# A four-layer conditioned transformer on one core: layer 0's value and output projections merged into one weight, one ScalarE pass per gelu and modulation, a Newton root, and a new order of steps

## The chip, the cores and the metric

The kernel runs on 1 core of one Trainium2 chip. The metric is device time in microseconds (us), the median of several executions. TensorE (PE) does matmuls and transposes into PSUM, VectorE (DVE), ScalarE (ACT) and GpSimd (POOL) work on tiles of 128 partitions, and SyncE (SP) issues the DMAs. Each engine works through its own queue in order and waits on semaphores.

## The reference

Four blocks follow each other on x of shape (4, 512, 256), each conditioned on a vector of 256 per batch. All have the same skeleton, in float32:

```python
def block(x, cond):                # layers 0..3 differ in norm, modulation, gates and heads
    h = modulate(norm(x), cond)    # scale and shift from cond @ W (+ bias)
    q, k, v = h @ Wq + bq, h @ Wk + bk, h @ Wv + bv
    p = softmax(q @ k.T * scale)   # layer 0: 1 head of 256; layers 1 to 3: 16 heads of 16
    x = x + gate * ((p @ v) @ Wp + bp)
    h = modulate(norm(x), cond)
    return x + gate * (gelu(h @ W1 + b1) @ W2 + b2)
```

Layer 0 has an rms norm and no gates. Layer 1 divides q and k by their norms (`x / max(sqrt(sum(x*x)), 1e-12)` over each head's 16 values) and scales q by exp(min(scale_mul, log 100)). Layer 3 has no FFN: its output is its second modulated norm added to x.

## The kernel before

A job is one batch of one layer, so there are 16 (`JOBS`): jobs 0 to 3 are layer 0, 4 to 7 layer 1, and so on. Weights and activations are kept as a rounded high part and the rest (`_h`, `_l`, type fp32r), and a product is three matmuls (`product`, L597 to L599: high by high, high by low, low by high). A few products stay in plain fp32, which TensorE does in two passes: `av0`, `av`, and the small modulation products.

All steps of all jobs stand in one list, `PLAN`, which `plan_steps` sorts by times written in tables (`SINGLE0`, `FFN`, `ATTN`, `LEAD_IN`, ...), in ticks counted from a job's start; a tick is four scores tiles of a unit of four heads. Every engine walks that list and issues its own part of each step, so the list fixes the order in each queue but not when a thing runs. In the windows of multi-head jobs (`multi_window`), the scores and row maxima stand in pairs, and `PAIR` and its kin say where in two ticks the `av` steps (A, or a and b) and the other steps (0 and 1) are put among them.

TensorE writes to a ring of seven PSUM banks (`RING`, `claim`), used in turn by every step of `RINGED`; a bank is claimed again when the engine that reads it has signalled. The eighth bank, `AVB`, holds the `av` sums of multi-head jobs.

What the change touches:
- `av0` and `proj` in layer 0. `pT0` transposes the probabilities into `oU`; `av0` (L729) makes (p v)^T, two tiles of 128x512; ScalarE (L916) rounds it into `postT_h` and VectorE (L1077) makes `postT_l`; `proj` multiplies by `wp`, and VectorE adds the result to X (L1242).
- `hT1`, `hT2`: four transposes, then ScalarE applies scale and shift twice from PSUM (L827), once in full (`hT_f`, `postT_f`) and once rounded (`hT_h`, `postT_h`), and POOL subtracts (L1301). `hT_f` lies in the memory of `hT_l`.
- `gelu`: for each of four tiles of `fc1`, ScalarE applies gelu twice from PSUM (L957, `gT_f` and `gT_h`), and POOL subtracts (L1306) and signals `g_lo`, for which `fc2a` and `fc2` wait.
- `qkroot` and `qkrs` in layer 1: VectorE clips the sums of squares (L1139), ScalarE takes the root (L861), VectorE the reciprocal (L1143) and the scaling of q (L1145).
- The row maxima of layers 2 and 3 (`max`, L1203) on VectorE, the exponentials (`scores`, L891 and L888) on ScalarE. ScalarE loads another function table whenever exp, gelu or sqrt follow each other.
- At the start VectorE splits the three pieces of layer 0's q, k and v weights itself (L1023, L1024; `EARLY`).

## Time and profile before

| what | value |
|---|---|
| three runs | 1158.63, 1163.27, 1162.45 us; median 1162.45 |
| profiled execution | span 1160.9 us from first to last instruction; its time outside the span is not listed apart |
| mean granted TensorE clock | 0.983 of full |
| busy in the span | TensorE 1094.3, ScalarE 800.4, VectorE 706.6, POOL 491.9 us |
| windows of 16 ticks | layer 0 with the lead-in 229.3 us; then 86.0, 84.0, 83.1, 73.9 (scores of layer 1); 84.1, 84.7, 83.0, 82.7 (layer 2); 82.6, 58.2, 58.5 (layer 3) and 70.8 to the end |

The windows are cut at the first scores matmul of each job. A window holds the attention of its job and the out projection and FFN of the job before, and the q, k and v of the job after. A matmul's row gives a modelled end, and neighbours overlap, so the distance from start to start tells what one costs TensorE. The name in a row is that of the tile; buffer numbers are left out.

### The profile page before, as it was taken

The numbers are of one execution on the slowest core, as the hardware profiler recorded it, in microseconds if no ns is written. First come the engines' busy times: TensorE is split into PE (matmuls) and PEld (weight loads), VectorE is DVE, ScalarE is ACT, GpSimd is POOL, SyncE is SP. The second block draws the span as 40 slices with busy tenths as digits, with TensorE's granted clock in tenths as the row PEclk, the third lists the DMA queues.
The fourth block names the chain that finished last, engine by engine and source line by source line (L and its number), as shares of the span: only waits on it lengthen the run. The fifth ranks groups of instructions, "written<-read, shape, count | busy, mean of one in ns | idle before, by whom it ended". The sixth has DMA issues, their size and how long they took to land.

```text
span 1160.9 us, 19685 instructions
## 1 busy us (share of the span) xinstructions
PE 1094.3 (94%) x6717; PEld 703.3 (61%) x6717; DVE 706.6 (61%) x1484; ACT 800.4 (69%) x1336; POOL 491.9 (42%) x447
## 2 busy tenths in 40 slices
PE   8899999889898999999999999999999999999985
PEld 5576877655555565656657656566656566555442
DVE  6554447535256266234775865865865866898874
ACT  3563655477788778787687686687687686686763
POOL 3542742613543623644335553335344345254222
PEclk9999999899999999999999999999999999999997
DMA  7000001213222203321122231023031121232301
GB/s 234 20 26 28 2 10 31 62 38 94 60 64 73 75 1 82 84 58 35 28 75 73 69 83 42 15 65 82 23 88 29 39 55 51 56 84 55 83 12 36
DMA packets 36385, 64.45 MB, mean 56 GB/s; under 512 B 7208, under 2 KB 22312, under 8 KB 36288
## 3 DMA queue, kind: packets, MB, share of 16 engines
q1 hardware_dynamic: 36288, 63.20, 20.6%
q8 instruction: 56, 0.92, 0.3%
q14 instruction: 41, 0.34, 0.1%
HBM read 22.90 MB, written 2.12 MB: 22 GB/s over the span
## 4 chain that ended last, share of the span: by engine, by line
PE 73%; DVE 10%; ACT 8%; issue 6%; POOL 4%; POOLq 0%; ACTq 0%; DVEq 0%
PE rings L597 13%; PE AVB L709 13%; PE rings L598 11%; PE rings L599 11%; PE rings L696 10%; PE rings L671 5%; DVE m L1203 2%; PE rings L729 2%; ACT probs L891 2%; PE rings L734 2%; PE rings L640 1%; ACT L891 1%; DVE m L1183 1%; ACT gT_h L957 1%; PE rings L746 1%
## 5 line engine op out<-in xcount | busy, mean ns | idle before, releaser
L1203 DVE TENSOR_REDUCE m<-rings 128x1 fp32r<-128x512 f32 x512 | 319.0, 681 | 100.6 <-PE rings L671 73.3
L891 ACT ACTIVATE probs<-rings 128x512 f32<-128x512 f32 x562 | 292.9, 616 | 99.4 <-PE rings L671 71.1
L696 PE MATMUL rings<-SQ,SK 64*128 64x512 f32 x768 | 237.9, 446 | 14.7 <-ACT probs L888 6.3
L671 PE MATMUL rings<-SK,SQ 63*128 63x512 f32 x512 | 200.3, 457 | 5.4 <-ACT probs L891 4.2
L696 PEld LDWEIGHTS rings<-SQ,SK 64*128 64x128 f32 x768 | 109.0, 188 | 142.4 <-issue 55.1
L709 PE MATMUL AVB<-probs,V 128*32 128x512 f32 x1536 | 193.6, 611 | 0.0
L1306 POOL TENSOR_TENSOR gT_l<-gT_f,gT_h 128x512 fp32r<-128x512 f32 x96 | 121.4, 1286 | 75.7 <-ACT gT_h L957 73.8
L888 ACT ACTIVATE probs<-rings 128x1024 f32<-128x1024 f32 x103 | 101.0, 1037 | 34.2 <-PE rings L696 20.6
L597 PE MATMUL rings<-w_h,gT_h 128*128 128x256 f32 x384 | 110.2, 287 | 1.2 <-ACT gT_h L957 0.7
L671 PEld LDWEIGHTS rings<-SK,SQ 63*128 63x128 f32 x512 | 84.2, 184 | 39.7 <-ACT probs L891 33.1
L598 PE MATMUL rings<-w_l,gT_h 128*128 128x256 f32 x384 | 106.7, 278 | 0.0
L599 PE MATMUL rings<-w_h,gT_l 128*128 128x256 f32 x384 | 106.7, 278 | 0.0
L957 ACT ACTIVATE gT_f<-rings,colv 128x512 f32<-128x512 f32 x96 | 66.9, 697 | 31.3 <-PE rings L599 28.6
L709 PEld LDWEIGHTS AVB<-probs,V 128*32 128x32 f32 x1536 | 39.5, 109 | 75.1 <-issue 59.8
L597 PE MATMUL rings<-postT_h,w_h 128*128 128x512 f32 x192 | 79.6, 415 | 3.5 <-ACT gT_h L957 2.4
L1301 POOL TENSOR_TENSOR postT_l<-postT_f,postT_h 128x512 fp32r<-128x512 f32 x24 | 31.4, 1310 | 115.4 <-ACT postT_h L827 115.1
L597 PEld LDWEIGHTS rings<-w_h,gT_h 128*128 128x128 f32 x384 | 72.3, 188 | 12.2 <-issue 7.3
L1340 POOL TENSOR_TENSOR tmp<-tmp,gates 128x512 f32<-128x512 f32 x32 | 41.1, 1285 | 86.0 <-DVE tmp L1270 44.9
L598 PE MATMUL rings<-postT_l,w_h 128*128 128x512 f32 x192 | 76.7, 399 | 0.0
L599 PE MATMUL rings<-postT_h,w_l 128*128 128x512 f32 x192 | 76.3, 398 | 0.0
L1301 POOL TENSOR_TENSOR hT_l<-hT_f,hT_h 128x512 fp32r<-128x512 f32 x30 | 38.6, 1290 | 86.7 <-ACT hT_h L827 86.6
L1270 DVE TENSOR_TENSOR tmp<-rings,rowp 128x512 f32<-128x512 f32 x40 | 27.5, 688 | 75.6 <-PE rings L599 75.5
(185 smaller groups left out, 2229.4 us busy)
## 6 DMA issues: line engine op xcount, KB each, us to landing
SQ<-qh SPq DMA_DIRECT2D x96, 128.0 KB, 2.6
SK<-kh SPq DMA_DIRECT2D x96, 128.0 KB, 2.8
SQ<-ql SPq DMA_DIRECT2D x48, 128.0 KB, 2.7
SK<-kl SPq DMA_DIRECT2D x48, 128.0 KB, 2.9
raw<-in_w SPq DMA_DIRECT2D x20, 256.0 KB, 2.8
wmod_s<-in_wmod SPq DMA_DIRECT2D x6, 512.0 KB, 4.1
gates<-gate_rows SPq DMA_DIRECT2D x12, 256.0 KB, 3.6
raw<-in_wqkv SPq DMA_DIRECT2D x9, 256.0 KB, 2.8
```

The source lines that it names most:

```text
L597: pe.matmul(out, sh, mh, start=first, stop=False)
L598: pe.matmul(out, sh, ml, start=False, stop=False)
L599: return pe.matmul(out, sl, mh, start=False, stop=last)
L671: mm = pe.matmul(o[:, :], SQ[a % 4][r:r + KS, n // 2, c * P:(c + 1) * P], SK[a % 4][r:r + KS, n // 2, :], start=True, stop=True)
L696: mm = pe.matmul(o[:, :], SK[a % 4][r:r + KS + 1, n // 2, c * P:(c + 1) * P], SQ[a % 4][r:r + KS + 1, n // 2, :], start=True, stop=True)
L709: mm = pe.matmul(AVB[32 * n:32 * n + 32, :], V[j % 2][:, i, (HD + 1) * h:(HD + 1) * h + 32], probs[:, (4 * t + n) % PROBS, :], start=(i == ...
L888: act.activation(probs[:, n % PROBS:n % PROBS + 2, :], two_banks(kind, a, i), ACT.Exp, scale=SCALE[layer(unit_job(a))]).then_inc(done["sco ...
L891: act.activation(probs[:, n % PROBS, :], bank(kind, a, i)[:, :], ACT.Exp, scale=SCALE[layer(unit_job(a))]).then_inc(done["scores"], 1)
L957: ins = act.activation(dst[:, m % (MT // 2), :], bank("fc1", a, m)[:, :], ACT.Gelu, bias=colv[:, layer(a), col:col + 1])
L1203: nc.vector.tensor_reduce(m16[:, col:col + 1], bank(kind, a, i)[:, :], AX_X, ALU.max, negate=True).then_inc(done["max"], 1)
L1301: nc.gpsimd.tensor_tensor(lo, full, hi.bitcast(F32), ALU.subtract).then_inc(done[kind], 1)
L1306: nc.gpsimd.tensor_tensor(gT_l[:, m, :], gT_f[:, m, :], gT_h[:, m, :].bitcast(F32), ALU.subtract).then_inc(g_lo, 1)
```

## The change

1. Layer 0 no longer multiplies p v by Wp. The third piece of its weights is loaded transposed, and a new step `merge` makes WvWp once (12 matmuls of 128x256, rounded by ScalarE, low part by VectorE) and puts it in Wv's place. `v` is then V WvWp, and `proj` multiplies the transposed probabilities by it (16 fp32 matmuls of 256 columns a job, 32 passes) and gives token-major output at once. `av0` goes. A step `mergerow` (8 passes) adds bv Wp to the bias row.
2. For layers 0 to 2 ScalarE makes only the full tile of hT and gelu. VectorE rounds it (`tensor_copy` to fp32r), and POOL's subtraction waits for that (`rounded`, `g_hi`). Layer 3 keeps both passes.
3. Layer 1's root is made on VectorE: an integer seed and three Newton steps, 12 instructions on 128x128 numbers, after which comes the scaling. Its scratch `root` lies in the memory of `tok1`, which is `kbar`'s too.
4. Until the first multi-head scores the ring has eight banks (`BANK`, `BEFORE`).
5. Every number in the tables of places is another one, so that steps stand elsewhere in the list everywhere.

```diff
+ROOT_SEED, ROOT_STEPS = 0x5f3759df, 3
...
-FFN = {"hT2": (23.5, 23.91), "fc1": (25.6, 25.81, 25.82, 25.83, 29.55, 29.56, 29.57, 29.58), "gelu": (25.84, 29.59),
-       "fc2a": (27.45, 29.55), "fc2": (30.55, 31.2)}
+FFN = {"hT2": (23.77, 23.78), "fc1": (24.07, 24.63, 24.66, 24.92, 28.07, 28.09, 28.15, 28.3), "gelu": (24.95, 29.13),
+       "fc2a": (26.1, 27.16), "fc2": (31.26, 32.12)}
...
+FIRST_SCORES = USE[("scores", UNITS * BATCH, 0)]
+BANK, BEFORE, _users = [], [], {}
+for _n, _s in enumerate(USES):
+    if _n < FIRST_SCORES:
+        BANK.append(_n % (RING + 1))
+    else:
+        BANK.append((_n - FIRST_SCORES) % RING)
+    BEFORE.append(_users.get(BANK[-1]))
+    _users[BANK[-1]] = _s
+    if _n == FIRST_SCORES - 1:
+        LAST_OF_EIGHTH = _users[RING]
...
+        def by_vector(a):
+
+            return layer(a) < LAYERS - 1
...
-                return ring[n % RING]
+                if BEFORE[n]:
+                    released(*BEFORE[n])
...
-                    pe.wait_ge(done["split_qkv"], nth("split_qkv", layer(a), part))
+                    if kind == "v" and layer(a) == 0:
+                        pe.wait_ge(done["merge"], 1)
+                    else:
+                        pe.wait_ge(done["split_qkv"], nth("split_qkv", layer(a), part))
...
-                elif kind == "av0":
-                    pe.wait_ge(done["pT0"], nth("pT0", a, TT - 1))
+                elif kind == "merge":
+
+                    pe.wait_ge(done["split_qkv"], nth("split_qkv", 0, 2))
+                    pe.wait_ge(done["split_wp"], 1)
+                    for c in range(CH):
+                        for k in range(CH):
+                            off = 2 * DIM + c * P
+                            mm = product(o[:, c * DIM:(c + 1) * DIM], [w[:, k, off:off + P] for w in (wqkv_h, wqkv_l)],
+                                         [w[:, k, :] for w in (wp_h, wp_l)], k == 0, k == CH - 1)
+                elif kind == "mergerow":
+
+                    pe.wait_ge(vb_ready, 1)
+                    pe.wait_ge(done["split_wp"], 1)
+                    for c in range(CH):
+                        for w in (wp_h, wp_l):
+                            mm = pe.matmul(o[:, 0:DIM], tok2[:, c, 0:P], w[:, c, :].bitcast(F32),
+                                           start=(c == 0 and w is wp_h), stop=(c == CH - 1 and w is wp_l))
+                elif kind == "proj" and not multi(a):
                     pe.wait_ge(done["v"], nth("v", a, 1))
-                    for t in range(TT):
-                        mm = pe.matmul(o[:, :], V[a % 2][:, t, i * P:(i + 1) * P], oU[:, t, :],
-                                       start=(t == 0), stop=(t == TT - 1))
+                    for t in range(2):
+                        pe.wait_ge(done["pT0"], nth("pT0", a, 2 * i + t))
+                        tok = (2 * i + t) * P
+                        for k in range(TT):
+                            mm = pe.matmul(o[:, t * DIM:(t + 1) * DIM], oU[:, k, tok:tok + P], V[a % 2][:, k, 0:DIM],
+                                           start=(k == 0), stop=(k == TT - 1))
                 elif kind == "oT1":
...
-                    for dst in (full[:, i, :], hi[:, i, :]):
+                    for dst in (full[:, i, :],) if by_vector(a) else (full[:, i, :], hi[:, i, :]):
                         ins = act.activation(dst, bank(kind, a, i)[:, :], ACT.Identity,
                                              bias=modb[:, l % 2, n, b:b + 1], scale=mods[:, l % 2, n, b:b + 1])
                     ins.then_inc(hi_in[kind], 1)
...
                     act.activation(sq[:, :], qk[:, i, :], ACT.Square).then_inc(sq_ready, 1)
-                elif kind == "qkroot":
-
-                    act.wait_ge(ss_ready, nth(kind, a))
-                    act.activation(rs[:, :, :], ss[:, :, :], ACT.Sqrt).then_inc(done[kind], 1)
...
-                elif kind == "av0":
+                elif kind == "merge":
                     act.wait_ge(pe_ring, use(kind, a, i))
-                    if a > 0 and i == 0:
-
-                        act.wait_ge(pe_ring, use(*POST_READ[(kind, a, i)]))
-                    act.activation(postT_h[:, i, :], bank(kind, a, i)[:, :], ACT.Identity,
-                                   bias=colv[:, 0, C_V + i:C_V + i + 1]).then_inc(hi_in[kind], 1)
+                    act.activation(wqkv_h[:, :, 2 * DIM:3 * DIM], bank(kind, a, i)[:, :].rearrange("p (c n) -> p c n", c=CH),
+                                   ACT.Copy).then_inc(hi_in[kind], 1)
                 elif kind == "av" and i == TT - 1:
...
-                        for dst in (gT_f, gT_h):
-                            ins = act.activation(dst[:, m % (MT // 2), :], bank("fc1", a, m)[:, :], ACT.Gelu,
-                                                 bias=colv[:, layer(a), col:col + 1])
-                        ins.then_inc(done["fc1"], 1)
+                        act.activation(gT_f[:, m % (MT // 2), :], bank("fc1", a, m)[:, :], ACT.Gelu,
+                                       bias=colv[:, layer(a), col:col + 1]).then_inc(done["fc1"], 1)
 
...
+                elif kind in ("hT1", "hT2") and by_vector(a) and (kind, a, i) not in EARLY:
+                    dve.wait_ge(hi_in[kind], nth(kind, a, i))
+                    full, hi = [x[:, i, :] for x in ((hT_f, hT_h) if kind == "hT1" else (postT_f, postT_h))]
+                    nc.vector.tensor_copy(hi, full).then_inc(rounded[kind], 1)
                 elif (kind, a, i) in EARLY and kind == "hT1":
                     dve.wait_ge(hi_in[kind], nth(kind, a, i))
+                    link(nc.vector.tensor_copy(hT_h[:, i, :], hT_f[:, i, :]))
...
-                elif kind in ("oT2", "av0"):
+                elif kind == "merge":
+                    dve.wait_ge(hi_in[kind], 1)
+                    nc.vector.tensor_tensor(wqkv_l[:, :, 2 * DIM:3 * DIM], bank(kind, a, i)[:, :].rearrange("p (c n) -> p c n", c=CH),
+                                            wqkv_h[:, :, 2 * DIM:3 * DIM].bitcast(F32), ALU.subtract).then_inc(done[kind], 1)
+                elif kind == "mergerow":
+                    dve.wait_ge(pe_ring, use(kind, a, i))
+                    dve.wait_ge(in_rowp, 16)
+                    nc.vector.tensor_tensor(rowp[:, R_PB:R_PB + DIM], bank(kind, a, i)[:, 0:DIM], rowp[:, R_PB:R_PB + DIM],
+                                            ALU.add).then_inc(done[kind], 1)
+                elif kind == "oT2":
                     dve.wait_ge(hi_in[kind], nth(kind, a, i))
...
 
                     dve.wait_ge(done["qkss"], nth("qkss", a, TT - 1))
-                    nc.vector.tensor_scalar(ss[:, :, :], ss[:, :, :], 1e-24, None, ALU.max).then_inc(ss_ready, 1)
-                elif kind == "qkrs":
-
-                    dve.wait_ge(done["qkroot"], nth("qkroot", a))
-                    link(nc.vector.reciprocal(rs[:, :, :], rs[:, :, :]))
+                    if nth(kind, a) > 1:
+                        dve.wait_ge(kbar_ready, nth("k", a - 1, CH - 1) - CH * BATCH)
+                    link(nc.vector.tensor_scalar(ss[:, :, :], ss[:, :, :], 1e-24, None, ALU.max))
+                    link(nc.vector.tensor_scalar(rs[:, :, :].bitcast(I32), ss[:, :, :].bitcast(I32), 1, None,
+                                                 ALU.arith_shift_right))
+                    link(nc.vector.tensor_scalar(rs[:, :, :].bitcast(I32), rs[:, :, :].bitcast(I32), -1, ROOT_SEED,
+                                                 ALU.mult, ALU.add))
+                    for _ in range(ROOT_STEPS):
+                        link(nc.vector.tensor_tensor(root[:, :, :], rs[:, :, :], rs[:, :, :], ALU.mult))
+                        link(nc.vector.scalar_tensor_tensor(out=root[:, :, :], in0=root[:, :, :], scalar=-0.5, in1=ss[:, :, :],
+                                                            op0=ALU.mult, op1=ALU.mult))
+                        link(nc.vector.scalar_tensor_tensor(out=rs[:, :, :], in0=root[:, :, :], scalar=1.5, in1=rs[:, :, :],
+                                                            op0=ALU.add, op1=ALU.mult))
                     dve.wait_ge(done["headscale"], 1)
                     nc.vector.tensor_tensor(rs[:, :, 0:HEADS], rs[:, :, 0:HEADS],
                                             smrow[:, :].unsqueeze(1).to_broadcast([P, TT, HEADS]), ALU.mult
                                             ).then_inc(done[kind], 1)
                 elif kind == "qknorm":
...
+                elif kind == "gelu":
+                    for m in range(MT // 2):
+                        dve.wait_ge(done["fc1"], nth("fc1", a, i * MT // 2 + m))
+                        nc.vector.tensor_copy(gT_h[:, m, :], gT_f[:, m, :]).then_inc(g_hi, 1)
...
-                    pool.wait_ge(hi_in[kind], nth(kind, a, i))
+                    if by_vector(a):
+                        pool.wait_ge(rounded[kind], nth(kind, a, i) - (CH if kind == "hT1" else 0))
+                    else:
+                        pool.wait_ge(hi_in[kind], nth(kind, a, i))
                     lo, full, hi = [x[:, i, :] for x in ((hT_l, hT_f, hT_h) if kind == "hT1" else (postT_l, postT_f, postT_h))]
                     nc.gpsimd.tensor_tensor(lo, full, hi.bitcast(F32), ALU.subtract).then_inc(done[kind], 1)
                 elif kind == "gelu":
 
                     for m in range(MT // 2):
-                        pool.wait_ge(done["fc1"], nth("fc1", a, i * MT // 2 + m))
+                        pool.wait_ge(g_hi, (nth(kind, a, i) - 1) * (MT // 2) + m + 1)
                         nc.gpsimd.tensor_tensor(gT_l[:, m, :], gT_f[:, m, :], gT_h[:, m, :].bitcast(F32), ALU.subtract
...
-        np.concatenate([g["L0_cond_q_w"], g["L0_cond_k_w"], g["L0_cond_v_w"]], axis=1),
+        np.concatenate([g["L0_cond_q_w"], g["L0_cond_k_w"], g["L0_cond_v_w"].T], axis=1),
         by_unit(g["L1_cond_mat_qkv_w"].T, 2), by_unit(g["L2_cond_Wqkv"], 2), by_unit(regroup(g["L3_cond_Wqkv"]).T, 2)])
```

TensorE in layer 0's first job. Before, `av0` (L729), v or k of the next job (L597 on hT, wqkv), and then the out projection, whose first product ends the piece:

```order
L729 MATMUL rings<-oU,V 128x512 x4
L597 MATMUL rings<-hT_h,wqkv_h 128x512
L598 MATMUL rings<-hT_l,wqkv_h 128x512
L599 MATMUL rings<-hT_h,wqkv_l 128x512
L597 MATMUL rings<-hT_h,wqkv_h 128x512
L598 MATMUL rings<-hT_l,wqkv_h 128x512
L599 MATMUL rings<-hT_h,wqkv_l 128x512
L597 MATMUL rings<-wp_h,postT_h 128x256
L598 MATMUL rings<-wp_l,postT_h 128x256
L599 MATMUL rings<-wp_h,postT_l 128x256
```

Now, at the same place of the job (L778 is `mergerow`, L786 the new `proj`, L762 `pT0`, L657 `modrow`):

```order
L676 MATMUL rings<-unit,tok_49 128x128 x4
L762 MATMUL rings<-unit,probs 128x128 x4
L657 MATMUL rings<-wmod_s,condS 4x512 x2
L778 MATMUL rings<-wp_h,tok 128x256
L778 MATMUL rings<-wp_l,tok 128x256
L778 MATMUL rings<-wp_h,tok 128x256
L778 MATMUL rings<-wp_l,tok 128x256
L786 MATMUL rings<-V,oU 128x256 x8
```

The rounded products by `wp` are gone; half of `proj` is eight fp32 matmuls of 256 columns.

ScalarE at the first gelu group of job 11, in the first window of layer 3's scores. Before:

```order
L891 ACTIVATE probs<-rings 128x512 x5
L957 ACT_TABLE_LOAD
L957 ACTIVATE gT_f<-rings,colv 128x512
L957 ACTIVATE gT_h<-rings,colv 128x512
L957 ACTIVATE gT_f<-rings,colv 128x512
L957 ACTIVATE gT_h<-rings,colv 128x512
L957 ACTIVATE gT_f<-rings,colv 128x512
L957 ACTIVATE gT_h<-rings,colv 128x512
L957 ACTIVATE gT_f<-rings,colv 128x512
L957 ACTIVATE gT_h<-rings,colv 128x512
L891 ACT_TABLE_LOAD
L891 ACTIVATE probs<-rings 128x512 x2
```

and now (L1003 is gelu, L855 a weight's high part, L899 v's copy, L941 the exponential):

```order
L941 ACTIVATE probs<-rings 128x512 x3
L1003 ACT_TABLE_LOAD
L1003 ACTIVATE gT_f<-rings,colv 128x512 x4
L855 ACTIVATE wp_h<-raw 128x512
L899 ACTIVATE V<-rings 128x16x16 x2
L941 ACT_TABLE_LOAD
L941 ACTIVATE probs<-rings 128x512 x8
```

Four gelu passes stand for eight between two table loads, and other copies stand before the second load.

VectorE at the same group. Before there was nothing of gelu in its queue (L1203 maxima, L1057 and L1060 statistics):

```order
L1102 TENSOR_SCALAR tok<-X,mv,rstd 128x256 x4
L1203 TENSOR_REDUCE m<-rings 128x1 x14
L1057 BN_STATS stats<-X 128x6 x4
L1060 BN_AGGR mv<-stats 128x2 x4
L1203 TENSOR_REDUCE m<-rings 128x1 x2
```

and now (L1278 maxima, L1067 and L1259 the rounding of hT2 and gelu, L1345 the FFN's result):

```order
L1278 TENSOR_REDUCE m<-rings 128x1 x6
L1067 CAST postT_h<-postT_f 128x512 x2
L1278 TENSOR_REDUCE m<-rings 128x1 x8
L1259 CAST gT_h<-gT_f 128x512 x4
L1278 TENSOR_REDUCE m<-rings 128x1 x2
L1285 CAST cT<-rings 16x64 x2
L1345 TENSOR_TENSOR tmp<-rings,rowp 128x512
```

The four casts, each waiting for one gelu tile, stand between the maxima, and the statistics have gone elsewhere.

## Rows read from the trace of the kernel before

**Rows 1.** Windows: busy time of each engine (instructions), clock, DMA, in four stretches.
```profile
core 0: us, PE busy (x) PEld busy (x) DVE busy (x) ACT busy (x) POOL busy (x), PEclk, DMA share, GB/s
0.00:229.30 229.30, 208.84 (x1091) 159.59 (x1091) 128.83 (x319) 114.14 (x197) 103.18 (x99) 0.98 0.17 51
229.30:315.30 86.00, 79.01 (x471) 49.24 (x470) 32.46 (x56) 65.04 (x91) 29.82 (x26) 0.94 0.24 64
...
556.30:640.40 84.10, 82.67 (x528) 52.22 (x524) 57.24 (x115) 63.16 (x112) 38.16 (x32) 1.00 0.23 61
...
890.80:973.40 82.60, 82.37 (x525) 52.05 (x526) 55.40 (x113) 60.26 (x106) 34.20 (x29) 1.00 0.16 39
```
**Rows 2.** The page, part 1: busy time of each engine over the span.
```profile
PE 1094.3 (94%) x6717; PEld 703.3 (61%) x6717; DVE 706.6 (61%) x1484; ACT 800.4 (69%) x1336; POOL 491.9 (42%) x447
```
**Rows 3.** Waits: who waited for whom, us in total, times, longest us.
```profile
PEld rings L696 <- DVE m L1203: 34.8, 71, 0.8
...
PEld rings L671 <- ACT probs L891: 33.1, 100, 0.9
```
**Rows 4.** Timeline of TensorE: start us, us, engine, line, count; rounded products and `av0`.
```profile
149.57 1.88 PE L729 MATMUL rings<-oU,V 128*128 128x512 f32 x4
...
944.49 0.28 PE L598 MATMUL rings<-w_l,gT_h 128*128 128x256 f32 x1
944.61 0.28 PE L599 MATMUL rings<-w_h,gT_l 128*128 128x256 f32 x1
```
**Rows 5.** Groups of ScalarE by form: busy us, mean ns | idle before.
```profile
L957 ACT ACTIVATE gT_h<-rings,colv 128x512 fp32r<-128x512 f32 x96 | 66.9, 697 | 0.0
...
L827 ACT ACTIVATE hT_h<-rings,modb,mods 128x512 fp32r<-128x512 f32 x32 | 25.5, 796 | 0.0
...
L827 ACT ACTIVATE postT_h<-rings,modb,mods 128x512 fp32r<-128x512 f32 x24 | 19.1, 797 | 0.0
...
L861 ACT ACT_TABLE_LOAD x4 | 5.1, 1283 | 0.1
```
**Rows 6.** Timeline around the first gelu group of job 11, three engines.
```profile
935.12 1.28 ACT L957 ACT_TABLE_LOAD   x1 [0.76 <-PE rings L599]
...
938.74 0.39 PE L599 MATMUL rings<-postT_h,w_l 128*128 128x512 f32 x1
...
940.42 0.73 ACT L957 ACTIVATE gT_h<-rings,colv 128x512 fp32r<-128x512 f32 x1
941.17 1.28 ACT L891 ACT_TABLE_LOAD   x1
...
941.48 1.29 DVE L1203 TENSOR_REDUCE m<-rings 128x1 fp32r<-128x512 f32 x2 [4.93 <-PE rings L671]
```
**Rows 7.** VectorE's SBUF operations alone and over POOL: a group, then timeline.
```profile
L1023 DVE CAST wqkv_h<-gT_f 128x512 fp32r<-128x512 f32 x3 | 1.3, 421 | 0.5 <-DMA gT_f<-in_wqkv 0.5
...
35.35 0.49 DVE L1223 TENSOR_SCALAR probs<-probs,small 128x512 f32<-128x512 f32 x1
...
36.65 1.28 POOL L1295 TENSOR_TENSOR wp_l<-gT_f,wp_h 128x512 fp32r<-128x512 f32 x1 [7.34 <-ACT wp_h L801]
...
36.84 1.38 DVE L1223 TENSOR_SCALAR probs<-probs,small 128x512 f32<-128x512 f32 x1
```
**Rows 8.** Groups of VectorE by form: layer 1's reciprocal and scaling.
```profile
L1143 DVE RECIPROCAL rs<-rs 128x128 f32<-128x128 f32 x4 | 3.8, 953 | 4.3 <-ACT rs L861 4.3
...
L1145 DVE TENSOR_TENSOR rs<-rs,rowh 128x64 f32<-128x64 f32 x4 | 0.9, 226 | 0.1
```
**Rows 9.** The first 20 us: DMA rate in 40 slices; VectorE's timeline.
```profile
GB/s 0 0 0 5 44 104 105 74 227 266 381 389 404 360 332 367 358 371 354 356 356 381 385 361 363 352 348 346 350 348 346 356 342 350 350 354 378 368 363 356
...
9.22 0.43 DVE L1023 CAST wqkv_h<-gT_f 128x512 fp32r<-128x512 f32 x1 [0.51 <-DMA gT_f<-in_wqkv]
...
11.62 0.17 DVE L1007 TENSOR_TENSOR modr<-rings,colv 128x16 f32<-128x16 f32 x1 [0.20 <-PE rings L626]
```
**Rows 10.** Timeline of VectorE near the end: `centre` between the finals.
```profile
1156.54 0.87 DVE L1110 SCALAR_TENSOR_TENSOR tok<-X,mv,gates 128x256 f32<-128x256 f32 x2
```

199 lines of the change are left out of this document (108 added, 91 removed), and 12 rows, old and new, of tables (FIRST, SINGLE0, START).

## The prediction

> **What bounds the kernel now.** I read the windows cut at the first scores matmul of each job first, since a share over the whole span mixes four layers. TensorE looks full everywhere [rows 1], and on the page it is busy for 1094.3 of 1160.9 us [rows 2]. That is not the floor: matmul ends are modelled and overlap. From start to start a 128x256 rounded product costs 0.12 us while its row says 0.28 [rows 4]. So I ask in each stage who holds PSUM banks. TensorE's weight loads show it: those of the scores wait 34.8 us for VectorE's row maxima, those of the maxima 33.1 us for ScalarE's exponentials, in steps of at most 0.9 us [rows 3]. The reader is to see three stages. Layer 0 (0 to 229.3): TensorE 208.8 of 229.3, ScalarE 114, VectorE 129; here matmul columns decide. Layer 1 (four windows, of which the first, 86.0 us long, stands in rows 1): ScalarE 65 busy, TensorE 79, VectorE only 32, so ScalarE is the partner that TensorE waits for. Layer 2 with the window after it (five windows; first and last stand in rows 1, 84.1 and 82.6 us): ScalarE 60 to 63 and VectorE 55 to 57; every probability tile needs one exponential and one maximum, so two partners pace the banks. The last 188 us have no FFN and keep their operations; only places change.
>
> **Layer 0, matmuls.** Each of four jobs loses 24 rounded 128x256 products (out projection; 2 tiles x 2 token blocks x 2 chunks x 3): 96 x 0.12 [rows 4] = 11.0 us at 0.115. `av0` had 64 passes of 512 columns at (1.88 - 0.59)/3 = 0.43 us [rows 4]; the new `proj` has 128 passes of 256 columns. No such form is in the trace. If a pass follows its columns it is 0.215 and the sum stays 27.5 us; if it kept the 0.43 of the long form it would be 27.5 us more; below, 0.12 like a rounded one, 12 us less. I take columns, since the rounded products do follow them. Added once: `merge`, 12 x 0.115 = 1.4, and `mergerow`, 8 passes x 0.22 = 1.7. Net -7.9 us, all on the path, since TensorE decides here.
>
> **Layer 0, start and waits.** VectorE now takes weight piece 2 (`split_qkv` 0.2) ahead of the first `mod`, and the SP queue loads the 512 KB of `load_mod` 0.1 ahead of that piece. The first piece landed at 9.2 us [rows 9]; 512 KB more and the piece itself, at about 360 GB/s [rows 9], are 2.1 us: 11.4, plus 1.1 for cast and subtraction, so `mod` starts near 12.5 where it started at 11.62 [rows 9]. The first h^T has one ScalarE pass less but a cast on VectorE, which takes that back in part: +0.5 us (bounds 0 and +3). The eighth bank while AVB rests, and `modrow` placed well ahead of `mod`, should give back some short waits: -1.5 (bounds +3, -5). Layer 0 in all: -9 us.
>
> **ScalarE.** 96 gelu passes of 0.697 (66.9 us) go, 24 of the 32 hT_h passes (19.1) and all 24 of the second norm (19.1) [rows 5]; eight `av0` copies go, one `merge` copy comes. Square roots leave with their four table loads [rows 5], and with other places the built order holds 45 loads for 50: 5 x 1.283 = 6.4 us. The Trainium skill (ScalarE: Activation LUTs, section What ACT_TABLE_LOAD costs) counts 2.66 us a switch, with a drain. By that rule five would be 13.3 us instead of 6.4. The trace shows 1.28 and 0.02 us before it [rows 6], so the row decides.
>
> In layer 1 a window loses on ScalarE 8 gelu passes at (941.15 - 936.40)/8 = 0.59 = 4.7 us (from the load at 935.12 + 1.28 to the last pass's end [rows 6]), four h^T passes at 0.80 = 3.2, and in three of four windows two loads = 2.6: 10.5, 10.5, 10.5, and 9.2 in the lead-in's. ScalarE is idle for 21 of 86 us there and TensorE for only 7 [rows 1], so not all of it is on the path: I take half, -20 us for the four windows. Bounds: nothing, and all of it, -41. The Newton root is neutral: before, 1.28 for the table, 0.95 for the reciprocal, and the root and its two hand-overs between them [rows 5, 8]; now 12 small VectorE instructions of about 0.23 each [rows 8] plus links, some 3.3 us, while that engine has 54 us idle in the first such window [rows 1].
>
> **VectorE, the price.** 144 roundings of 128x512 arrive (96 gelu, 48 h^T). Alone such a cast takes 0.42 us. But a SBUF-to-SBUF operation of VectorE that overlaps a POOL one stretches: the same scaling of probs took 0.49 alone and 1.38 over two POOL subtractions, and ended 0.29 after the first of them [rows 7]. Since POOL subtracts the low half right behind each cast, the second to fourth cast of a gelu group meet it: 60 us in all if none do, 199 if each costs 1.38; I take 110. The Trainium skill says why (SBUF — State Buffer, section SBUF: two separate sides): the pair of ports is an exclusive lock for a whole instruction. The row agrees.
>
> In layer 2 I follow one gelu group [rows 6]. fc1's last matmul ends at 939.13; ScalarE, two passes behind, finished at 941.15, loaded exp's table and had exponentials at 942.46. With one pass it would finish at 939.8 and have exponentials at 941.1: 1.4 earlier. VectorE however stands in its queue at the casts until the last has waited for POOL, about 941.2, against a first maximum at 941.48: 0.3 earlier. So 0.3 to 1.4 per group, I take 0.8; two groups x five windows = -8 us. Behind the waiting casts in VectorE's queue are the maxima, and for their banks TensorE waits; that is the cover that may be gone (rival B). The four h^T casts I set against the four ScalarE passes: zero, bounds -3 and +5 a window.
>
> **The rest.** Layer 3 keeps ScalarE's two passes; 0 (bounds +4, -4). At the end `centre` 15.2 and 15.3 (0.87 us [rows 10]) stand ahead of the reciprocal root's end instead of between the finals: -0.9.
>
> **Sum.** -9 - 20 - 8 - 0.9 = -38. From the profiled span of 1160.9 (the execution's own total is not listed apart) to 1123; the median of the three runs is 1162.45, 1.5 above the span, so 1125 us. Own range 1110 to 1145.
>
> **Rivals.** (A) More comes back: ScalarE's whole relief reaches the end. Layer 1 -41, layer 2 with both terms full (1.4 x 10 + 3 x 5 = -29, taken at -20), layer 0 -9 : 1160.9 - 70 = 1091, with the 1.5 some 1093 (1080 to 1110). For it: over 110 us of ScalarE go (66.9 + 19.1 + 19.1 + 6.4), and shorter av pieces stand between score blocks; against: VectorE has as much to do in layer 2.
> (B) VectorE becomes the bound in layer 2: slower. Place: the casts in the five windows with maxima. Price: 12 casts x 1.38 = 16.6 us a window; hidden are the some 4.9 us which VectorE idled by a group before [rows 6], twice: 9.9. Left +6.7 x 5 = +33; the casts of layer 1 eat half its gain (-10 left), layer 0 gives -9: 1160.9 + 14 + 1.5 = 1176. It decides from about 5.8 us a window on the path, where it eats layer 0's and 1's -29. For it: the bank waits on maxima are already the largest [rows 3]; against: the casts fall where it idled.
> (C) TensorE's own sequence covers the gelu passes: only matmuls and some places count, 1150 (1145 to 1156).
> (D) The places cost what the operations give (a weight piece split before it landed, SP held by an early `stack`): same, 1162.
>
> **Chances.** Forecast 0.47, A 0.20, C 0.10, D 0.08, B 0.15. About 0.5% (6 us) is what a measurement of this kernel tells from no change. Faster is the forecast, A and C: 0.77; same 0.08; slower 0.15. The range 1092 to 1166 leaves out B and A's lower half.
>
> **What the profile will show.** Right: first score matmul of layer 1 near 220 (before 229.3); layer 1 windows near 79; layer 2 windows near 81 with ScalarE near 52 and VectorE near 67; new fp32 passes 0.215 apart; casts between 0.42 and 1.4. What would make the forecast wrong: passes 0.43 apart (layer 0 longer), TensorE's loads waiting for the casts by tens of us (B), layer 1 windows unchanged (C), or waits on weight DMAs at ScalarE (D).

## The result, and the profile after

The kernel after takes 1110.3 us (median of four runs, 1107.1 to 1111.1) against 1162.9 before on the same chip: ratio 0.954, interval 0.952 to 0.957. Forecast was 1125 with a range of 1110 to 1145: the sign was right, and the gain was 52 us where 38 was said. The median lies 0.3 us inside the lower end of that range, which is also the upper end of rival A's; two of the four executions lie below it. Its profiled execution spans 1105.3 us, 55.6 less than that of before.

The windows of the kernel after, cut at the first scores matmul of each job from layer 1 on, answer to [rows 1]; columns are length, busy time of PE, weight load, DVE, ACT, POOL with their instructions, TensorE's granted clock, DMA share and GB/s.

```profile
0.00:207.90 207.90, 197.88 (x1091) 161.06 (x1091) 151.24 (x361) 87.71 (x153) 105.55 (x97) 0.99 0.16 50
207.90:284.30 76.40, 72.50 (x484) 46.91 (x484) 49.66 (x84) 54.60 (x71) 36.84 (x30) 1.00 0.26 67
...
514.10:596.90 82.80, 79.87 (x525) 50.40 (x526) 68.05 (x129) 55.39 (x97) 37.82 (x31) 1.00 0.22 58
...
840.90:921.40 80.50, 79.43 (x522) 51.21 (x520) 63.97 (x124) 55.63 (x97) 34.57 (x29) 1.00 0.18 44
```

Layer 0 is 21.4 us shorter than before, the first layer-1 window 9.6, the first window of layer 2 1.3 and the last 2.1. In layer 0 TensorE's time outside its busy rows fell from 20.5 to 10.0 us, and its busy time by 11.0: with 7.9 us of columns forecast, more than half of what layer 0 gave is not matmul columns. VectorE has 151 us of work in layer 0 where it had 129.

The first part of the page answers to [rows 2], and the waits of TensorE's weight loads to [rows 3].

```profile
PE 1055.9 (96%) x6705; PEld 689.8 (62%) x6705; DVE 833.9 (75%) x1663; ACT 709.0 (64%) x1181; POOL 503.5 (46%) x447
```
```profile
PEld rings L732 <- DVE m L1278: 57.3, 101, 1.2
...
PEld rings L707 <- ACT probs L941: 11.6, 45, 0.7
```

ScalarE lost 91 us, VectorE got 127. The reader is to see the partner change: waits of the maxima's loads for ScalarE went from 33.1 to 11.6 us, those of the scores' loads for VectorE rose from 34.8 to 57.3. VectorE is the next one to meet, but TensorE's loads wait for its maxima for at most 1.2 us at a time.

The groups by form show the rounding (line 1259 for gelu, 1067 for the modulation), GpSimd's subtraction behind it and the new fp32 products; columns are busy us, mean ns of one, idle before. The line of TensorE's timeline below has start and length of 16 of these products.

```profile
L1259 DVE CAST gT_h<-gT_f 128x512 fp32r<-128x512 f32 x96 | 82.5, 888 | 57.3 <-ACT gT_f L1003 56.0
...
L1067 DVE CAST postT_h<-postT_f 128x512 fp32r<-128x512 f32 x24 | 18.7, 781 | 7.3 <-ACT postT_f L881 7.1
L1067 DVE CAST hT_h<-hT_f 128x512 fp32r<-128x512 f32 x22 | 18.6, 859 | 8.3 <-ACT hT_f L881 8.3
...
L1384 POOL TENSOR_TENSOR gT_l<-gT_f,gT_h 128x512 fp32r<-128x512 f32 x96 | 129.8, 1375 | 111.7 <-DVE gT_h L1259 111.7
...
L786 PE MATMUL rings<-V,oU 128*128 128x256 f32 x128 | 29.0, 380 | 0.0
```
```profile
79.25 3.62 PE L786 MATMUL rings<-V,oU 128*128 128x256 f32 x16
```

The casts take 119.8 us in all (110 was forecast). The fp32 passes start (3.62 - 0.38)/15 = 0.216 us apart (0.215 forecast). Of the other signs that the forecast named, the layer-1 windows average 76.6 us (near 79 was said), those of layer 2 81.5 (near 81) with VectorE at 64 to 68 (near 67), but ScalarE stands at 55 to 58 in them, not near 52.

How the lengths of the stages moved in every kernel that was run is the table on which most of what follows rests. Each is summed from windows cut as above. "Old places" are the tables of before with the new steps put in, "new places" those of the kernel after. The runs were made on several chips, so a median is best compared by its ratio to before on the same chip. The stages are those of the one profiled execution, which for the kernel after was its fastest and for two_passes and seven_banks their slowest. Kernels that share the steps behind layer 0 (after, seven_banks, extra_products) differ there by up to 2.0 us in layer 1, 2.8 in layer 2 and 1.0 in the rest, so a difference of that size between stages says nothing. Two executions of root_new_places were slow (1410 and 3328 us); its median here is that of the other four.

| kernel | median us | ratio to before (95%) | layer 0 | layer 1 (4) | layer 2 (5) | rest |
|---|---|---|---|---|---|---|
| before | 1162.9 | 1 | 229.3 | 327.0 | 417.1 | 187.5 |
| merge_old_places | 1162.4 | 0.998 (0.996 to 1.000) | 225.7 | 328.8 | 417.1 | 190.5 |
| root_old_places | 1160.1 | 0.996 (0.995 to 0.998) | 231.8 | 328.7 | 410.6 | 188.5 |
| two_passes_old_places | 1166.4 | 1.003 (1.0015 to 1.0045) | 229.2 | 333.6 | 417.2 | 188.9 |
| old_places | 1170.4 | 1.006 (1.004 to 1.008) | 233.2 | 336.2 | 410.5 | 188.9 |
| layer0_places | 1150.8 | 0.989 (0.987 to 0.991) | 209.6 | 342.5 | 410.5 | 189.2 |
| later_places | 1141.8 | 0.981 (0.979 to 0.984) | 239.2 | 304.8 | 407.6 | 182.9 |
| two_passes | 1131.5 | 0.974 (0.971 to 0.976) | 209.9 | 320.1 | 416.5 | 185.5 |
| gelu_twice | 1123.7 | 0.966 (0.964 to 0.968) | 207.7 | 311.3 | 419.5 | 183.0 |
| extra_products | 1120.8 | 0.964 (0.962 to 0.967) | 218.2 | 307.1 | 410.1 | 184.8 |
| seven_banks | 1116.4 | 0.960 (0.957 to 0.964) | 218.1 | 305.1 | 409.0 | 184.9 |
| root_new_places | 1108.6 | 0.953 (0.951 to 0.956) | 209.6 | 303.0 | 409.0 | 184.4 |
| gelu_low_vector | 1109.5 | 0.954 (0.951 to 0.956) | 208.4 | 305.1 | 408.9 | 184.4 |
| after | 1110.3 | 0.954 (0.952 to 0.957) | 207.9 | 306.2 | 407.3 | 183.9 |

### The profile page after: what moved, and what is told of

Same layout as the page of the kernel before. It is cut to its first block, busy times and chain, and to the rows that moved or that the text cites. A ratio compares the mean times of both kernels' runs of the same rounds, so it can differ in the third digit from the quotient of the medians.

```text
span 1105.3 us, 19686 instructions
## 1 busy us (share of the span) xinstructions
PE 1055.9 (96%) x6705; PEld 689.8 (62%) x6705; DVE 833.9 (75%) x1663; ACT 709.0 (64%) x1181; POOL 503.5 (46%) x447
## 3 DMA queue, kind: packets, MB, share of 16 engines
q1 hardware_dynamic: 36288, 63.20, 21.4%
## 4 chain that ended last, share of the span: by engine, by line
PE 70%; DVE 16%; issue 5%; POOL 3%; ACT 3%; DMA 1%; SPq 1%; DVEq 0%; POOLq 0%; ACTq 0%
PE rings L630 13%; PE rings L632 11%; PE rings L631 11%; PE rings L747 11%; PE rings L732 10%; DVE m L1278 4%; PE rings L707 4%; PE rings L786 2%; PE rings L676 2%; POOL gT_l L1384 2%; PE rings L791 1%; PE rings L657 1%; PE rings L803 1%; DVE gT_h L1259 1%; DVE m L1254 1%
## 5 line engine op out<-in xcount | busy, mean ns | idle before, releaser
L941 ACT ACTIVATE probs<-rings 128x512 f32<-128x512 f32 x572 | 302.7, 607 | 120.0 <-PE rings L707 67.0
L1278 DVE TENSOR_REDUCE m<-rings 128x1 fp32r<-128x512 f32 x512 | 316.3, 678 | 12.3 <-PE rings L707 10.1
L747 PE MATMUL rings<-probs,V 128*32 128x512 f32 x1536 | 196.5, 607 | 0.0
L707 PE MATMUL rings<-SK,SQ 63*128 63x512 f32 x512 | 189.1, 450 | 1.1 <-ACT probs L941 0.6
L1384 POOL TENSOR_TENSOR gT_l<-gT_f,gT_h 128x512 fp32r<-128x512 f32 x96 | 129.8, 1375 | 111.7 <-DVE gT_h L1259 111.7
L1259 DVE CAST gT_h<-gT_f 128x512 fp32r<-128x512 f32 x96 | 82.5, 888 | 57.3 <-ACT gT_f L1003 56.0
L938 ACT ACTIVATE probs<-rings 128x1024 f32<-128x1024 f32 x98 | 96.3, 1034 | 24.5 <-issue 12.0
L707 PEld LDWEIGHTS rings<-SK,SQ 63*128 63x128 f32 x512 | 84.0, 185 | 15.9 <-ACT probs L941 11.6
L1003 ACT ACTIVATE gT_f<-rings,colv 128x512 f32<-128x512 f32 x96 | 62.3, 687 | 34.2 <-PE rings L632 32.7
L747 PEld LDWEIGHTS rings<-probs,V 128*32 128x32 f32 x1536 | 36.2, 109 | 70.6 <-issue 63.0
L631 PEld LDWEIGHTS rings<-w_l,gT_h 128*128 128x128 f32 x384 | 73.1, 190 | 0.2
L632 PEld LDWEIGHTS rings<-w_h,gT_l 128*128 128x128 f32 x384 | 73.0, 190 | 0.0
```

Of the source, the lines that this page charges most:

```text
L631: pe.matmul(out, sh, ml, start=False, stop=False)
L632: return pe.matmul(out, sl, mh, start=False, stop=last)
L707: mm = pe.matmul(o[:, :], SQ[a % 4][r:r + KS, n // 2, c * P:(c + 1) * P], SK[a % 4][r:r + KS, n // 2, :], start=True, stop=True)
L747: mm = pe.matmul(AVB[32 * n:32 * n + 32, :], V[j % 2][:, i, (HD + 1) * h:(HD + 1) * h + 32], probs[:, (4 * t + n) % PROBS, :], start=(i == ...
L938: act.activation(probs[:, n % PROBS:n % PROBS + 2, :], two_banks(kind, a, i), ACT.Exp, scale=SCALE[layer(unit_job(a))]).then_inc(done["sco ...
L941: act.activation(probs[:, n % PROBS, :], bank(kind, a, i)[:, :], ACT.Exp, scale=SCALE[layer(unit_job(a))]).then_inc(done["scores"], 1)
```

## Experiments

**The new operations at the old places** (old_places): the tables of before, with the few steps that are new put in by hand. Only this one choice of places for them was run.

```diff
-SINGLE0 = {"stat1": (-2.7,), "norm1": (-31.14,), ...
+SINGLE0 = {"stat1": (-16.2,), "norm1": (-23.7,), ... "proj": (10.18, 10.73), ... "bias": (9.5,)}
-FIRST = {...}
+FIRST = {("merge", 0, 0): 1.35, ("mergerow", 0, 0): 6.5, ("v", 0, 0): 3.1, ("v", 0, 1): 3.5, ...
```

> All new operations (merge, one ScalarE pass with VectorE rounding, Newton root, eight banks), but every step at the places of before; only merge, mergerow, layer 0's v, split_wp, bias 0 and proj had to be put anew. Theory O (operations): the 55 us come from what the engines no longer do, the places give about 10: 1118 to 1128 us. Theory P (places): the new order fills TensorE's waits and the operations alone give only the matmuls and a little: 1140 to 1152 us.

Measured: 1170.4 us, 0.6% slower than before and 60 us slower than after. Both ranges that stood on record are missed, the upper one by 18 us. The operations at these places gave nothing; the gain appears only with the new order. The waits of TensorE in this kernel (total us, times, longest) say where it went:

```profile
PE rings L686 <- DVE qk L1214: 14.2, 4, 3.9
PE rings L621 <- POOL postT_l L1370: 6.1, 3, 4.0
PE rings L711 <- DVE m L1245: 5.1, 4, 4.0
```

Once in each of four jobs TensorE stands for the normalised q and k of layer 1. VectorE's timeline at the third of them shows the root's chain, and TensorE's the wait:

```profile
346.22 0.23 DVE L1195 TENSOR_SCALAR ss<-ss 128x128 f32<-128x128 f32 x1
...
349.94 0.23 DVE L1207 TENSOR_TENSOR rs<-rs,rowh 128x64 f32<-128x64 f32 x1
350.20 2.50 DVE L1214 TENSOR_TENSOR qk<-qk,rs 128x512 f32<-128x512 f32 x4
```
```profile
352.84 1.94 PE L686 MATMUL rings<-unit,qk 128*128 128x128 f32 x8 [3.57 <-DVE qk L1214]
```

From 346.22 to 349.94 the root takes 3.7 us, with GpSimd idle from its third step on, and TensorE, which had run out of other work, waits 3.57. Windows 2 and 3 of layer 1 also show a low clock, which makes their matmuls longer:

```profile
317.10:406.00 88.90, 80.06 (x491) 49.89 (x490) 52.15 (x104) 56.70 (x77) 39.59 (x34) 0.92 0.24 62
406.00:494.50 88.50, 80.74 (x495) 50.58 (x494) 51.56 (x105) 55.50 (x76) 38.51 (x33) 0.92 0.22 57
```

Much of the low clock stands right behind these waits. Three stretches around the wait above, columns as before:

```profile
340.00:350.00 10.00, 9.27 (x64) 5.16 (x64) 7.03 (x24) 8.74 (x15) 5.74 (x6) 1.00 0.08 26
350.00:360.00 10.00, 7.16 (x39) 5.90 (x39) 9.13 (x18) 5.56 (x10) 2.12 (x2) 0.66 0.01 2
360.00:370.00 10.00, 9.50 (x52) 5.51 (x49) 5.73 (x9) 8.96 (x12) 4.29 (x4) 1.00 0.73 172
```

From 352 to 358 the granted clock is 0.50, the lower level of 1.2 GHz. After the other two waits in layer 1, 3.94 us up to 266.80 and 3.75 up to 441.21, it is 0.66 (265 to 270) and 0.52 (440 to 445). So such a wait costs more than its own length: the clock that is missing from 350 to 360 is worth another 3.4 us (0.34 x 10; an estimate, full only if TensorE's work decides all of that stretch).

**ScalarE's second passes at the new places** (two_passes): gelu and the modulation are computed twice again.

```diff
-            return layer(a) < LAYERS - 1
+            return False
...
-                        act.activation(gT_f[:, m % (MT // 2), :], bank("fc1", a, m)[:, :], ACT.Gelu, ...
+                        for dst in (gT_f, gT_h):
+                            ins = act.activation(dst[:, m % (MT // 2), :], bank("fc1", a, m)[:, :], ACT.Gelu, ...
```

> The changed kernel with ScalarE's second passes back: gelu, hT1 and hT2 are written twice by ScalarE and VectorE rounds nothing; places, merge, root and banks as changed. Theory O: the 28 us of layers 1 and 2 go back, 1134 to 1142 us. Theory P: the order carries it, 1113 to 1122 us. A third view, that VectorE's casts cost as much as ScalarE's passes: 1105 to 1113 us.

Measured: 1131.5, between the ranges of theories O and P, so at these places the rounding is worth 21 us by medians. The table has 13.9 in layer 1, 9.2 in layer 2, 2.0 in layer 0 and 1.6 in the rest, 26.7 in all: it sets the slowest execution of one kernel against the fastest of the other, so the stages are some 5 us too high together. The loads' waits for VectorE's maxima were 48.4 us with two passes and 57.3 with one, those for ScalarE 20.1 and 11.6: the same exchange as against before.

**Without the eighth bank** (seven_banks): the ring stays at seven banks in layer 0 too.

```diff
-        BANK.append(_n % (RING + 1))
+        BANK.append(_n % RING)
```

> The changed kernel with seven banks before the first multi-head scores too. If the eighth bank is what recovered the 10 us of TensorE's idle time in layer 0 beyond the forecast: 1117 to 1121 us. If the places did it: 1109 to 1112 us.

Measured: 1116.4, 6.0 us more (by medians; the profiled executions lie 11.8 apart, since one was at the fast end of its runs and one at the slow end). Layer 0 is 10.2 longer: 6.7 us are time in which TensorE is not busy, and 3.5 are longer busy time, at a granted clock of 0.95 from 150 us on where the kernel after has 1.00. TensorE's waits there are now for single results that hold a bank:

```profile
PE rings L630 <- DVE tmp L1343: 3.1, 1, 3.1
PE rings L784 <- DVE m L1252: 2.8, 1, 2.8
```

In layer 0 of the kernel after the first of these is 0.3 us and the second does not appear. The clock is low behind the first: TensorE starts again at 159.71, and from 160 to 165 the clock is 0.66.

**96 products put back** (extra_products): six further rounded 128x256 products ahead of each new out projection's block, overwritten by it.

```diff
+                        for n in range(6):
+                            pe.matmul(o[:, t * DIM:(t + 1) * DIM], unit[:, :], wp_h[:, n % CH, :], start=True, stop=True)
```

> The changed kernel with 24 more 128x256 rounded matmuls per job of layer 0 in proj (their result is overwritten), as many as the out projection had. If TensorE's columns decide layer 0, each costs 0.115 us: +11 us, 1121 us. If the products were hidden behind other engines: +0 to +4, 1110 to 1114 us.

Measured: 1120.8, +10.5 us for 96 x 0.115 = 11.0; layer 0 is 10.3 longer (218.2 for 207.9). Nothing hides columns there, so in the new order the step of the prediction that put the saved products wholly on the path holds. At the old places it does not hold in full (merge_old_places, below).

**The root on ScalarE, new places** (root_new_places).

```diff
-                    link(nc.vector.tensor_scalar(rs[:, :, :].bitcast(I32), ss[:, :, :].bitcast(I32), 1, None,
-                                                 ALU.arith_shift_right))
...
+                    dve.wait_ge(root_done, nth(kind, a))
+                    link(nc.vector.reciprocal(rs[:, :, :], rs[:, :, :]))
```

> The kernel after at its own places, with the root of layer 1 taken back: ScalarE takes four square roots of 128 x 64 and its tables are loaded again around them, VectorE takes a reciprocal in place of eleven small steps. The prediction took the root as neutral. Theory 1 (the root costs as much on VectorE as it frees on ScalarE): within 6 us of the kernel after (1110), so 1104 to 1116. Theory 2 (the fewer table loads on ScalarE, about 1.3 us each, give back what the chain of eleven steps takes and more, as the order was made for it): 1116 to 1125. Theory 3 (the chain of eleven small steps on VectorE, near 6 us in front of the q and k of each job, is now a brake, as the longest wait of TensorE in layer 1 on VectorE's normalised q and k, 3.2 us at L695, has it): below 1104.

Measured: 1108.6, the same as after (intervals 0.951 to 0.956 and 0.952 to 0.957). The root is neutral here, though not for the reason given. In the kernel after the chain is not 3.3 us. VectorE's timeline in layer 1's third job:

```profile
301.27 0.22 DVE L1204 TENSOR_SCALAR ss<-ss 128x128 f32<-128x128 f32 x1
301.52 1.23 DVE L1205 TENSOR_SCALAR rs<-ss 128x128 int32<-128x128 int32 x1
302.79 1.21 DVE L1207 TENSOR_SCALAR rs<-rs 128x128 int32<-128x128 int32 x1
304.03 1.40 DVE L1210 TENSOR_TENSOR tok<-rs 128x128 f32<-128x128 f32 x1
...
308.08 0.22 DVE L1216 TENSOR_TENSOR rs<-rs,rowh 128x64 f32<-128x64 f32 x1
```

It takes 6.8 us, because three of its small steps fall beside GpSimd and take 1.2 to 1.4 instead of 0.23 to 0.29. Each ends 0.08 to 0.14 us after the GpSimd operation beside it; two of these are

```profile
301.39 1.28 POOL L1425 TENSOR_TENSOR X<-X,tmp 128x512 f32<-128x512 f32 x1
302.63 1.28 POOL L1418 TENSOR_TENSOR tmp<-tmp,gates 128x512 f32<-128x512 f32 x1
```

Behind this chain TensorE waits 2.80 us, up to 312.68, and from 315 to 320 its clock is 0.53. In all it waits 6.2 us for q and k in the kernel after (three times, up to 3.2 us at line 695). With the root back it does not wait for them at all, but 3.9 us for ScalarE's exponentials (line 733; 0.4 in the kernel after), with 52 table loads for 45. So one wait stands for another; that they weigh the same is read from the time, not from the waits.

```profile
PE rings L733 <- ACT probs L942: 3.9, 6, 1.7
PE rings L631 <- POOL gT_l L1380: 3.3, 5, 0.8
```

**The root on ScalarE, old places** (root_old_places): the same edit on old_places.

> The new operations at the old places (1170.4, against 1162.8 before), with the root of layer 1 back on ScalarE. At these places TensorE waited 11.3 us in layer 1 (three times, up to 3.9) for VectorE's normalised q and k. Theory 1 (the chain of small steps of the root, put at places made for a single square root, is what makes layer 1 longer there): layer 1's four windows go from 336 back to about 326 and the time to 1158 to 1163. Theory 2 (the root is neutral there too, and what lengthens layer 1 is VectorE's rounding queued ahead of the norm): 1167 to 1173.

Measured: 1160.1, 10.3 us less than old_places; layer 1 goes from 336.2 to 328.7, and the wait for q and k from 14.2 to 4.3 us:

```profile
PE rings L687 <- DVE qk L1210: 4.3, 4, 1.2
```

So the chain of small steps is what made layer 1 longer at the old places; theory 1 of this run. At the place of the wait shown above TensorE now waits 1.04 us, and its clock stays at 1.00 from 330 to 370.

**Two passes at the old places** (two_passes_old_places): the edit of two_passes on old_places.

> The new operations at the old places, but with ScalarE's second pass of gelu and of the modulation back in place of VectorE's rounding. At the new places these second passes cost 21 us. Theory 1 (at the old places the rounding gives nothing or harms, since VectorE's queue has it ahead of work that TensorE waits for): 1162 to 1171, no slower than with the rounding (1170.4). Theory 2 (the rounding is worth near 20 us at any places, and something else of the new operations costs that much at the old ones): 1185 to 1195.

Measured: 1166.4, 4.0 less than with the rounding (ratios 1.0015 to 1.0045 against 1.004 to 1.008, which just meet). At the old places, with the root on VectorE, the rounding gives nothing and by the medians harms a little. The table splits it: layer 2 is 6.7 us longer without it, layers 0 and 1 are 4.0 and 2.6 shorter, and the two spans differ by 0.1, so that only the medians carry the 4.0.

**Gelu alone twice** (gelu_twice), new places: only the second part of two_passes' edit.

> The kernel after at its own places, with gelu alone computed twice by ScalarE again (96 x 0.70 us more on ScalarE, 96 x 0.89 us less on VectorE); the modulation keeps VectorE's rounding. Both together cost 21 us. Theory 1 (each group's gain goes by its share of ScalarE's time, gelu 67 of the 112 us that were taken away): 1121 to 1125. Theory 2 (it is the modulation's latency ahead of the products that counts, not gelu's): 1112 to 1116. Theory 3 (all of it is gelu, whose eight passes stand between the products of a feed-forward): 1128 to 1132.

Measured: 1123.7. Of the 21 us gelu's rounding gives 13.4 and the modulation's 7.8: near their shares of ScalarE's time (theory 1). In layer 2, whose first window is below, it costs 12.2 us over five windows (two_passes has 9.2 for both, so these two agree only within some 3 us), and ScalarE is 4.8 us busier in it than after:

```profile
519.00:603.90 84.90, 81.50 (x525) 51.90 (x526) 61.90 (x121) 60.16 (x105) 36.82 (x31) 0.98 0.21 56
```

**New places for layer 0 alone** (layer0_places) and **for the rest alone** (later_places): complementary halves of the tables.

```diff
 # layer0_places: new SINGLE0 to SINGLE3, FFN0 to FFN2, FIRST, NEXT1, LEAD_IN and START; all others old
 # later_places: the other way round
```

> The new operations, with the new places for layer 0 alone (its single jobs, its first three feed-forwards, the start, what is done in it for layer 1, and the lead-in to layer 1), and the old places for all that follows. Theory 1 (the places work where they stand, stage by stage): the stretch to the first layer-1 scores is near 208 as in the kernel after instead of 233, the rest stays near 935 as at the old places, so a time near 1145 (1140 to 1150) against 1170.4 and 1110.3. Theory 2 (an order is worth what it is only as a whole: the work that layer 0's new order pushes out comes back behind it): the first stretch ends near 208 too, but layer 1 grows by over 8 us and the time is over 1153.

> The complement: the new operations, the old places for layer 0, and the new ones for layers 1 to 3. Theory 1 (additive, stage by stage): 233 to the first layer-1 scores, then near 897 as in the kernel after, so a time near 1135 (1130 to 1140); with the run before this one the two gains of 25 and 35 us then add to the 60 us between the old and the new places. Theory 2 (not additive): below 1128 or above 1143.

Measured: 1150.8 and 1141.8. Neither lies in a range on record; layer0_places is 0.8 above that of theory 1, later_places 1.8 above. The lengths away from the seam are those of the whole kernels: layer 2 of layer0_places 410.5 as in old_places, of later_places 407.6 as after (407.3). At the seam something is lost. The window behind it in layer0_places:

```profile
209.60:301.80 92.20, 83.40 (x484) 54.52 (x484) 46.35 (x84) 55.88 (x74) 32.36 (x27) 0.90 0.27 73
```

is 8.3 us longer than at the old places, with one wait of 5.5 us for the DMA of SQ:

```profile
PE rings L725 <- DMA SQ<-cT: 5.5, 1, 5.5
```

The wait took the place of others: outside its busy rows TensorE has 8.8 us in this window and 8.2 at the old places. What is longer is its busy time, 83.4 for 75.7, at a clock of 0.90 for 0.98. Layer 0 of later_places is 6.0 longer (239.2 for 233.2). So neither "additive" nor "given back" is right as it was put: 1.8% and 2.5% make 4.3 of the 5.2% between old_places and after, and what is missing was lost at the seam, where two orders meet that were not made for one another. For later_places the profiled execution, 1136.3, fits the additive theory and the median does not; I call that run unclear by itself.

**Gelu's low half on VectorE** (gelu_low_vector), new places:

```diff
-                        nc.vector.tensor_copy(gT_h[:, m, :], gT_f[:, m, :]).then_inc(g_hi, 1)
+                        link(nc.vector.tensor_copy(gT_h[:, m, :], gT_f[:, m, :]))
+                        nc.vector.tensor_tensor(gT_l[:, m, :], gT_f[:, m, :], gT_h[:, m, :].bitcast(F32), ALU.subtract
+                                                ).then_inc(g_lo, 1)
```

> The kernel after at its own places, but the low half of gelu's output (gelu minus its rounded value) is subtracted by VectorE right behind the rounding, and not by GpSimd: GpSimd loses 96 passes of 1.375 us, VectorE gets 96 more. Theory 1 (the rounding takes 0.89 us on the mean and not 0.42 because GpSimd's subtractions run beside it and the two share something; with them gone it takes 0.42, the subtraction takes 0.5 and VectorE is 15 us busier at most, while the products of the second half of the feed-forward get their low half sooner): 1103 to 1111, and the rounding's mean near 0.5 in the trace. Theory 2 (VectorE's queue is what counts: 96 passes more in front of the maxima that TensorE waits for, each 0.5 to 1.1 us): 1120 to 1150.

Measured: 1109.5, the same as after. The groups say that the premise on the casts was right:

```profile
L1260 DVE TENSOR_TENSOR gT_l<-gT_f,gT_h 128x512 fp32r<-128x512 f32 x96 | 71.1, 741 | 3.3
L1259 DVE CAST gT_h<-gT_f 128x512 fp32r<-128x512 f32 x96 | 43.3, 451 | 48.2 <-ACT gT_f L1003 48.1
```

The cast falls from 888 to 451 ns, and VectorE is only 14.5 us busier (848.4) for 96 more operations, while GpSimd loses 125. The trade buys no time and costs none. It does not tell what shorter casts would give by themselves, since 96 subtractions stand in VectorE's queue in their place: a cast and its subtraction are 1.19 us together where a cast was 0.89, and the loads' waits for VectorE's maxima went from 57.3 to 62.6 us. To let VectorE round straight from PSUM was not tried.

**Merge and eighth bank alone, old places** (merge_old_places): both edits above on old_places.

> The old places, with of the new operations only layer 0's products by V WvWp and the eighth bank: the root is on ScalarE and gelu and the modulation have their second pass, as in the kernel before. With root and rounding new as well the time is 1170.4; with the root alone taken back 1160.1, with the passes alone taken back 1166.4. Theory 1 (the two effects add: the root costs 10.3 at the old places and the rounding 4.0, each whatever the other is): 1156 (1153 to 1159), so the rounding harms even with the root on ScalarE, and merge and eighth bank give some 7 us. Theory 2 (they do not add: the rounding harmed only because its passes and the root's chain stand in one queue of VectorE; without that chain it gives something): above 1160, up to 1166.

Measured: 1162.4. On this base the rounding alone changes -2.3 us, the root alone +4.0, both together +8.0 where the sum would be +1.7. By the ratios to before it is -2, +6 and +9. So the effects do not add (theory 2), but the excess of 6 us has about 4 us of uncertainty from the four intervals. That both stand in VectorE's one queue is the likely cause and not shown: TensorE's wait for q and k in layer 1 is 11.3 us with the rounding and 11.2 without it (two_passes_old_places).

Against before, merge and eighth bank shorten layer 0 by 3.6 us. TensorE's busy time there fell from 208.8 to 201.9, near the 7.9 that were forecast for the columns, but its time outside the busy rows grew from 20.5 to 23.8. At these places part of what the columns gave went into waits.

## Why the prediction was right, and where it was not

**Layer 0, -9 forecast, -21.4 measured: mis-sized.** The term "short waits -1.5" failed, not the matmuls. The products are on the path at 0.109 us each (extra_products: 10.5/96) and the new fp32 passes follow their columns. But the eighth bank, named inside that term, is worth 6.0 us by medians and 10.2 in layer 0's own window. Of the 20.5 us that TensorE was not busy in layer 0 [rows 1] the forecast gave back 1.5; at the new places the eighth bank alone takes 6.7 us of such time away (218.1 - 201.4 = 16.7 with seven, 10.0 with eight). At the old places the bank and the products together shorten layer 0 by 3.6 us only. No run has one of them without the other there, so how the bank pays in that order stays open. "All on the path, since TensorE decides here" was thus a property of the new order, and not of the layer.

**Start, +0.5.** The delay came, and larger than the +0.9 that the forecast worked out for `mod`, which starts 1.7 us later than before (11.62):

```profile
13.34 0.18 DVE L1054 TENSOR_TENSOR modr<-rings,colv 128x16 f32<-128x16 f32 x1 [0.63 <-PE rings L662]
```

But between 20 and 40 us TensorE is busy 19.9 us where it was 16.7, so the delay was taken back at once.

**Layer 1, -20 forecast, -20.8 measured.** The size is right, the ground in part. With the two passes back at the new places the layer is 320.1, and before it was 327.0: the rounding gives 13.9, or some us less since its profiled execution is its slowest, and the places with the root on VectorE the rest of the 20.8. At the old places the rounding gives nothing there (328.8 and 328.7, both with the root on ScalarE), and the root on VectorE costs 7.5. "Half of ScalarE's relief" thus hit a sum of two terms by luck, of which the forecast had one.

**Layer 2, -8 forecast, -9.8 measured: right in size, and the rounding is its cause, but not by the path that was forecast.** At the old places the layer is 417.1, 417.1 and 417.2 us in the three kernels with two passes and 410.5, 410.5 and 410.6 in the three with one, all at a granted clock of 1.00: 6.6 us, which need no special order. At the new places it is 9.2, where the clock of two_passes is 0.99. A gelu group of the kernel after, to be set beside [rows 6]:

```profile
885.34 1.28 ACT L1003 ACT_TABLE_LOAD   x1 [0.52 <-PE rings L632]
886.64 2.07 ACT L1003 ACTIVATE gT_f<-rings,colv 128x512 f32<-128x512 f32 x3
889.40 0.69 ACT L1003 ACTIVATE gT_f<-rings,colv 128x512 f32<-128x512 f32 x1 [0.69 <-PE rings L632]
```
```profile
887.36 0.43 DVE L1259 CAST gT_h<-gT_f 128x512 fp32r<-128x512 f32 x1 [2.03 <-ACT gT_f L1003]
887.94 1.85 DVE L1259 CAST gT_h<-gT_f 128x512 fp32r<-128x512 f32 x2 [0.15 <-ACT gT_f L1003]
890.12 1.10 DVE L1259 CAST gT_h<-gT_f 128x512 fp32r<-128x512 f32 x1 [0.34 <-ACT gT_f L1003]
891.25 1.29 DVE L1278 TENSOR_REDUCE m<-rings 128x1 fp32r<-128x512 f32 x2
```

ScalarE has done its passes 4.8 us after the load's start, where it took 6.0. It now waits for fc1 and not the other way round. VectorE's casts lie where it would idle, and its first maximum starts 5.9 us after the load where it was 6.4. The exponentials gained nothing in this group: 7.4 us after the load, 7.3 before (892.75 and 942.46), because two copies of V and a weight split now stand ahead of them on ScalarE:

```profile
889.99 0.62 ACT L855 ACTIVATE wp_h<-raw 128x512 fp32r<-128x512 f32 x1
890.78 0.66 ACT L899 ACTIVATE V<-rings 128x256 f32<-128x256 f32 x2 [0.18 <-PE rings L632]
...
892.75 0.60 ACT L941 ACTIVATE probs<-rings 128x512 f32<-128x512 f32 x1
```

The time that gelu freed in this group went to other work of ScalarE, moved there by the order, and not to exponentials that start 0.8 us earlier as the prediction had it. Over the five windows TensorE's own waits for exponentials (line 707) are 0.6 us, where two_passes has 3.8 and 2.0 more for gelu. So the relief shows where TensorE met ScalarE, though not at the step that was counted.

**Layer 3 and the end, -0.9 forecast, -3.6 measured.** Places alone: the rest is 187.5 to 190.5 us in the six kernels that have it at the old places and 182.9 to 185.5 in the eight that have it at the new. Which step did it was not tested.

**The root, "neutral".** Right at the new places and wrong as a property of the change: +10.3 us at the old places beside the rounding, +4.0 without it. Its length, 3.3 forecast, is 3.7 alone and up to 6.8 beside GpSimd.

**The rivals.** B (VectorE the bound in layer 2) falls: layer 2 is shorter with the casts than without, in both orders. A's range ends at 1110, 0.3 us from the time, but its mechanism is not what the runs show: it wanted -41 and -20 from layers 1 and 2, which gave -20.8 and -9.8, and the time came so low by layer 0, where A had the same -9 as the forecast. Its "over 110 us of ScalarE go" adds the lengths of rows that overlap: the passes are 105 us by that sum, and ScalarE's busy time differs by 80.0 (789.0 in two_passes, 709.0 after). C's count of columns is right for its own term and misses the eighth bank and layers 1 and 2. D's causes did not show; that the operations alone leave the time nearly the same, as in old_places, is a different thing, for there the new places are missing.

**What the step-by-step count could not see** is how much the order is worth by itself. With two passes, the new order is worth 34.9 us (1166.4 to 1131.5); with one, 60.1 (1170.4 to 1110.3); the 25 us between are the rounding's, -21 in the new order and +4 in the old. I had priced places alone at -0.9 and a few waits. The single prices at the new places (rounding 21.2, products 10.5, bank 6.0, root nothing) add up to 38 of the 52 us; no run has all the old operations in the new order, so that the other 15 are the order's own is an estimate which takes these prices as additive. Part of the order's worth is the clock: its mean was 0.976 in old_places and 0.989 after, which over the spans is 56 and 24 us of TensorE at its lower level of 1.2 GHz (twice the missing share times the span), and at most half of the difference, 16 of the 60 us, can be lost to it. Between the two kernels with two passes (0.976 and 0.979) it is at most 4 of the 35. No run changed the clock alone; in old_places it was low behind the long waits for q and k, and where the root's return made such a wait short it stayed at 1.00. So most of what the order gives is not clock, and the part that is follows at least in these places from waits that the order makes.

## What to carry to other kernels

When work is moved from one engine to another, price the queue that it joins as well as the queue that it leaves: the same rounding and root together cost 8 us in the old order, and in the new one the rounding brought 21 us and the root cost nothing. So judge an operation in an order that fits it, and cross operations and orders before dropping either. A chain of small dependent steps belongs where TensorE has other work for the whole length of the chain, GpSimd's interference included. A wait of several us of TensorE is to be priced with the low clock behind it. One more PSUM bank is worth a try where TensorE is the bound and still not busy all the time.

## What the runs showed of the hardware

- A 128x512 cast of VectorE takes 0.43 us alone and 0.89 on the mean beside GpSimd's subtraction; when that subtraction leaves GpSimd the mean is 0.45. It also holds for small operations: a 128x128 int32 step took 0.23 us alone (old_places) and 1.23 beside a GpSimd operation of 128x512, 0.08 us past that one's end (after).
- The other side is lengthened less: GpSimd's subtraction in gelu took 1375 ns on the mean with the casts beside it and 1286 in the kernel before, which has none.
- VectorE's subtraction of two fp32 tiles of 128x512 in SBUF takes 0.74 us, GpSimd's 1.375, so the low half costs less on VectorE in engine time, though here it gained nothing.
- Behind waits of TensorE of 2.8 to 3.9 us the granted clock was low for some us: 0.50 from 352 to 358 behind 3.57 us (old_places), 0.53 from 315 to 320 behind 2.80 (after), 0.66 from 160 to 165 behind 3.1 (seven_banks). Behind a wait of 1.04 at the same place of the order it stayed at 1.00 (root_old_places), and so it did for 7 us behind one of 2.95 that ended at 192.76 (old_places).
- An fp32 pass of 256 columns starts 0.216 us after the one before; six rounded 128x256 products more per block cost 0.109 each on the end.
